# Attention on TensorE: the first transposes of a row block's probabilities in front of the product with v of the block before

## The reference

```python
q, k, v = x @ w_q.T, x @ w_k.T, x @ w_v.T            # per batch: 1024 x 128 each
q_rot, k_rot = _rotate(q, cos, sin), _rotate(k, cos, sin)
scores = einsum('bqd,bkd->bqk', q_rot, k_rot) / sqrt(128)
scores = where(causal, scores, -inf)
attn = softmax(scores, axis=-1)
x = x + einsum('bqk,bkd->bqd', attn, v)
```

## Time and profile before

| | |
|---|---|
| median of 3 runs | 815.38 us (814.73 to 815.74) |
| profiled execution | 816.33 us, its span 814.5 us |
| mean granted clock of TensorE | 0.999 |
| TensorE, matmul busy | 802.5 us (99%) |
| TensorE, weight loads busy | 657.1 us (81%) |
| VectorE busy | 722.9 us (89%) |
| GpSimd busy | 615.2 us (76%) |
| ScalarE busy | 600.1 us (74%) |

### The profile page before, as it was taken

One profiled execution on the slowest core, in us unless ns is written; L12 is line 12 of the kernel. 1 busy time (PEld: TensorE's weight loads), 2 busy tenths in 40 slices (PEclk: granted clock), 3 DMA queues, 4 the chain that ended last, 5 costly groups with the idle time before them and its releaser, 6 DMA issues. The chain is left out here.

```text
span 814.5 us, 15848 instructions
## 1 busy us (share of the span) xinstructions
PE 802.5 (99%) x4066; PEld 657.1 (81%) x4066; DVE 722.9 (89%) x2027; ACT 600.1 (74%) x1495; POOL 615.2 (76%) x560
## 2 busy tenths in 40 slices
PE   8999999999999999999999999999999999999998
PEld 7677777777778767899999998777777777777887
DVE  6899999999999988788888888789999999999986
ACT  5777788888786677776676766778788778886664
POOL 6777777777777679888888884477777777777764
PEclk9999999999999999999999999999999999999999
DMA  7567788878877746643333450556676776666653
GB/s 231 137 175 210 211 246 237 243 233 243 219 207 209 206 123 163 159 140 83 100 96 112 145 150 20 159 148 188 183 201 194 195 202 197 179 177 173 184 143 94
DMA packets 93480, 140.83 MB, mean 173 GB/s; under 512 B 10352, under 2 KB 39648, under 8 KB 93408
## 3 DMA queue, kind: packets, MB, share of 16 engines
q1 hardware_dynamic: 93408, 140.03, 61.6%
HBM read 112.67 MB, written 18.93 MB: 162 GB/s over the span
## 5 line engine op out<-in xcount | busy, mean ns | idle before, releaser
L633 POOL TENSOR_TENSOR h_l<-probT,h_h 128x512 fp32r<-128x512 f32 x254 | 330.0, 1302 | 137.4 <-ACT h_h L857 135.1
L857 ACT ACTIVATE h_h<-probT 128x512 fp32r<-128x512 f32 (+1 forms) x285 | 179.4, 629 | 58.2 <-DVE probT L1326 28.6
L1798 PE MATMUL bank<-xh,w_h 128*128 128x512 f32 x545 | 218.7, 401 | 2.4 <-DVE prob L1316 1.4
L1798 PE MATMUL bank<-xh,w_l 128*128 128x512 f32 x545 | 214.2, 393 | 0.0
L1798 PE MATMUL bank<-xl,w_h 128*128 128x512 f32 x545 | 213.8, 392 | 0.0
L920 ACT ACTIVATE bank<-bank 128x512 f32<-128x512 f32 x252 | 146.2, 580 | 68.5 <-PE bank L1798 65.9
L1326 DVE TENSOR_TENSOR probT<-prob,bank 128x512 f32<-128x512 f32 x255 | 172.6, 677 | 15.3 <-POOL h_l L633 3.6
L1316 DVE TENSOR_TENSOR prob<-bank,qkT 128x512 f32<-128x512 f32 x252 | 171.3, 680 | 15.6 <-ACT bank L920 11.2
L1798 PEld LDWEIGHTS bank<-xh,w_h 128*128 128x128 f32 x545 | 102.3, 188 | 40.5 <-DVE probT L1329 7.2
L1798 PEld LDWEIGHTS bank<-xh,w_l 128*128 128x128 f32 x545 | 102.3, 188 | 23.3
L1798 PEld LDWEIGHTS bank<-xl,w_h 128*128 128x128 f32 x545 | 102.3, 188 | 21.2
(11 more groups left out here) (143 smaller groups left out, 1340.5 us busy)
## 6 DMA issues: line engine op xcount, KB each, us to landing
qkT<-comb_rows SPq DMA_DIRECT2D x190, 256.0 KB, 5.2
qkT<-comb_rows SPq DMA_DIRECT2D x124, 128.0 KB, 3.0
rows<-comb_rows SPq DMA_DIRECT2D x28, 512.0 KB, 7.1
stage<-stage SPq DMA_DIRECT2D x64, 128.0 KB, 3.0
X<-in_x SPq DMA_DIRECT2D x16, 256.0 KB, 3.1
stage<-in_x_t SPq DMA_DIRECT2D x16, 256.0 KB, 6.7
x_t<-stage SPq DMA_DIRECT2D x16, 256.0 KB, 4.5
X<-x_rows SPq DMA_DIRECT2D x64, 64.0 KB, 5.8
```

What stands on the lines that cost most here:

```text
L633: nc.gpsimd.tensor_tensor(lo, f, hi.bitcast(F32), ALU.subtract).then_inc(done, 1)
L857: return nc.scalar.activation(dst, src, ACT.Copy)
L1798: return nc.tensor.matmul(dst, lhsT, rhs, start=start, stop=stop)
```

## The change

The call that transposes the first group of block i moves from behind the product of block i-1 (and behind `ffn_prep`, in batch 7) to before it. Nothing changes on the other engines.

```diff
                     if first and i >= 1:
                         pe.wait_ge(v_done, (i - 1) // 2 + 1)
+                    attn_probT(b, i, 0, last)
                     if i >= 1:
                         attn_pv(b, p, i - 1)
                     elif not first:
                         attn_pv(b - 1, 1 - p, QB - 1)
                     if last:
                         ffn_prep(i)
-                    attn_probT(b, i, 0, last)
                     if i >= 1:
                         for item in before:
                             attn_item(item, b + 1, 1 - p)
```

## The result

The changed kernel takes 841.28 us (median of 4 runs, 840.56 to 842.09) against 815.38 us (814.73 to 815.74): 25.9 us slower, ratio 1.032 (95% interval 1.0304 to 1.0337). The forecast was 844.7 us, range 836 to 850.

What follows compares the result with a forecast made beforehand. TensorE was taken to set the pace. New waits of 3.93 us a batch gave 23.6 us in six batches, plus 2.7 in batch 0 and 3.0 in batch 7: 29.3 us over 815.38, forecast 844.7 us, range 836 to 850.

Steps and rivals of the forecast that it cites:

- (b): Rival: TensorE's clock falls to 1.2 GHz for the work of each step 7, giving 867 us; chance 0.03.
- (c): Rival: TensorE's waits for residual and copy go and nothing takes their place, giving 812.0 us; chance 0.03.
- (d): Rival: no change, losses and gains cancel or the exponentials move forward as much, giving 815 us; chance 0.03.
- step 0: Block 0's transposes, behind block 1's scores, wait for their exponentials: 0.84 us a batch.
- step 1: Block 1's stretch: copy wait replaced by waits for the residual and the next input's low half, net 0.07 us.
- step 4: Block 4's transposes, behind block 5's scores, wait for their exponentials: 0.24 us a batch.
- step 5: Block 5's transposes, behind block 6's scores, wait for their exponentials: 0.72 us a batch.
- step 6: Block 6's transposes wait for their exponentials: 0.54 us a batch, bounds 0.25 and 0.75.
- step 7: Block 7's transposes, behind the shortest scores, wait for the longest exponentials: 1.20 us a batch.
- The early first copy: ScalarE's first copy done during the product, so exponentials start earlier: 0.2 us in step 6, under 0.1 in step 7.
- rival (a): Exponentials come earlier than old offsets, small waits vanish: 2.1 us a batch, some 16 us, giving 831; chance 0.08.
- a_i: Moment when step i of a batch loads the first weights of block i+1's scores; exponentials' offsets count from it.

## Why the prediction was right

**The cause** was as stated: the product of block i-1 was the cover of the exponentials, and ahead of it the scores alone are too short. Steps, cover and exponentials were each changed by themselves, and the time followed each time. The rivals (b) to (d) are excluded: the clock is 1.00, and the entries of the earlier trace rows did go, as (c) has it, but they were worth 3.4 us, 2.2 us came back as the wait for the low half, and the new waits are some 30 us. (d) falls with the result.

**The steps of one batch**, forecast and measured: step 0, 0.84 and 0.95; step 1, 0.07 and 0.11; step 2, 0.11 and 0.02; step 3, 0.21 and 0.19; step 4, 0.24 and 0.24; step 5, 0.72 and 0.69; step 6, 0.54 and 0.38; step 7, 1.20 and 1.17. Sum 3.93 and 3.75.

**The mis-sized terms.** The early first copy moves the exponentials of step 6 from 1.95 to 425.63 - 423.95 = 1.68 us behind a_6, 0.27 and not 0.20, and those of step 7 to 1.43 and not 1.50. Against that the 0.06 us from the exponentials to the transposes is 0.12 in the loop of batches 1 to 4, inside the stated bounds; it is 0.05 outside. So rival (a) was right in its direction and far too large in size: the second copy still waits for its transposes.

**A term that the sum did not have.** It takes the loss of a step for its wait. But behind a wait the same loads go through a little faster. In step 6, from the first load behind the scores to the next scores' load, they took 2.68 us before (413.70 to 416.38) and take 2.52 now (425.75 to 428.27). The wait's own terms give 1.68 + 0.12 - 1.26 = 0.54 us, exactly the forecast; the 0.16 us caught up leave 0.38. In step 7 it is 0.04 us (2.43 and 2.39). Step 0 goes the other way, by 0.09 (1.89 and 1.98).

**What the working had wrong about the offsets.** It says that they hold in the next step, and by its formula step 1 would wait 1.18 + 0.06 - 0.48 = 0.76 us for the exponentials of block 1. It leaves this term out without a reason. That was right by luck: with step 0 changed, block 0's transpose, its copy and the exponentials of block 1 are no longer behind the product, and the offset falls from 1.18 to 0.03 us. In the kernel with steps 1 to 4 alone, where it does not fall, the transposes of step 1 wait 0.83 us. The recorded sign of being wrong, exponentials that move forward by more than 0.2 us against a_i, did occur, in steps 1 (1.15) and 6 (0.27). It hardly moved the sum: step 1 had been counted at 0.07, and step 6 with 0.20 of it.

**How much of the closeness is luck.** With the loop written out the gap is 0.05 to 0.06 us in batches 1 to 7, as good as the forecast's 0.06. One batch there (403.80 to 430.90) takes 27.10 us, 3.20 more than before and not 3.93: by steps 0.75, 0.11, -0.03, 0.17, 0.17, 0.63, 0.30 and 1.10. The whole span is 837.2 us, in one execution 22.7 more than before, where the forecast had 29.3. The loop's longer gap (2.0 us) and the late projection below (1.0 us) bring the changed kernel's span to 25.8. So the mechanism and the order of the steps were right, the sum was more than a quarter too high, and two things that were not foreseen closed half of the distance.

**The batches.** Batch 0 from its second step on lost 2.3 us (forecast 2.7), batches 1 to 6 lost 21.6 (23.6; from the scores' load at 349.37 to that at 514.51 it is 165.14 us, against 347.42 to 490.92, 143.50), batch 7 and the start of the next stage 2.2 (3.0); the rest of the span is 0.3 us shorter ahead of the stage. That makes the 25.8 us. Batch 5, outside the loop, lost less than those in the loop: 26.89 us against 27.54 to 27.65. Batch 6 took 27.87 us, and there is a single event in it: GpSimd got the swapped halves of a projection late,

```profile
497.87 1.29 POOL L799 TENSOR_TENSOR rope_s<-stage,sin 128x512 f32<-128x512 f32 x1 [5.37 <-DMA stage<-stage]
```

and the exponentials awaited in step 4 ended about 1 us later against its scores than elsewhere; step 4 took 4.35 us, where batch 5 has 3.37. In the kernel with the loop written out that wait is shorter in the same place (3.30 us) and step 4 takes 3.37, though TensorE's order is the same, and the kernel with the earlier exponentials has one step 4 of the same length (4.32 us) in another batch; so I take it for a matter of single executions. It was not tried further.

**Range and forecast.** 841.28 lies 3.4 us below the forecast, most of it the six inner batches at 0.3 us each and the two outer ones.

## What to carry to other kernels

When two pieces of work on the bounding engine are swapped, ask first what the first one was hiding. For each wait that moves forward, take the end of what it waits for relative to the start of the step, subtract what still stands in front, and add up the steps; here that gave 29.3 us from one batch's rows, where 25.8 were traced, and 22.7 without the loop's longer gap and one late projection. Check each step's offset again once the step before it has changed; step 1 shows why. An engine order that looks idle-free can be a match of two orders: TensorE's and ScalarE's have to be changed together, and even then a third order remains: here VectorE's row maximum stood behind a rotation that waited for a copy which ScalarE now made later.

## What the runs showed of the hardware that I had not expected

In TensorE's hardware loop the transposes, which have two semaphore waits in a row, loaded 0.12 to 0.13 us behind the event that released them; with the loop written out it was 0.05 to 0.06 us, in the same batches. In the loop too it was 0.05 to 0.06 us in the two kernels where one of the waits was already passed, so the longer gap is not one of every wait in a loop; which of the two waits makes it stays open. It only shows where the wait is not covered. Most of these loads have "issue" as their releaser in the wait view, so an "issue" entry can be a wait for another engine.

Behind such a wait of the weight loads the loads that follow went through up to 0.16 us faster than without it (step 6), so that the waits of a step add up to somewhat more than the step loses.
